# Moving the z gate's products ahead of the candidate's in a slot-attention GRU on one Trainium2 core

## What is computed

```python
for _ in range(3):
    sn = rmsnorm(slots, slot_norm_w)
    scores = einsum('bkd,bmd->bkm', sn @ Wq.T, k_proj) * SCALE
    attn = softmax(scores, axis=-2)
    attn = attn / (sum(attn, axis=-1, keepdims=True) + EPS)
    updates = einsum('bkm,bmd->bkd', attn, v_proj)
    gx, gh = updates @ wih.T + bih, slots @ whh.T + bhh
    r, z = sigmoid(xr + hr), sigmoid(xz + hz)
    n = tanh(xn + r * hn)
    slots = (1 - z) * n + z * slots
```

## Time and profile before

| | |
|---|---|
| median of 3 runs | 638.34 us (637.24 to 638.39) |
| profiled execution | 638.83 us |
| its span, first to last instruction | 637.1 us |
| PE busy | 546.8 us, 86% |
| PE weight load busy | 402.8 us, 63% |
| DVE busy | 457.4 us, 72% |
| ACT busy | 373.3 us, 59% |
| POOL busy | 253.5 us, 40% |
| mean granted TensorE clock | 0.922 |

### The profile page before, as it was taken

The page is one execution under the profiler, slowest core; times in us unless marked ns, Lnnn a source line. Parts: engine busy times, 40 slices in busy tenths (PEclk is TensorE's granted clock), DMA queues, the critical chain, the costliest instruction groups (busy, mean ns, idle before and its releaser), DMA issues.

```text
span 637.1 us, 7357 instructions
## 1 busy us (share of the span) xinstructions
PE 546.8 (86%) x2158; PEld 402.8 (63%) x2158; DVE 457.4 (72%) x806; ACT 373.3 (59%) x661; POOL 253.5 (40%) x239
## 2 busy tenths in 40 slices
PE   6999897597799979997997999799989886858781
PEld 3474536265578857876785788578878764636560
DVE  3999899985894995799489758964756579653431
ACT  4558195865665846584666668475756544634542
POOL 1032302021042564456454744543443462554453
PEclk9999897679899989998999999899999997878776
DMA  8921003010110000000000000020110724145421
GB/s 296 329 82 66 1 0 132 0 68 0 67 66 1 1 1 1 1 0 1 1 0 1 1 1 1 1 66 24 42 51 26 254 102 125 69 127 141 121 77 34
DMA packets 23896, 37.88 MB, mean 59 GB/s; under 512 B 3246, under 2 KB 15663, under 8 KB 23601
## 3 DMA queue, kind: packets, MB, share of 16 engines
q1 hardware_dynamic: 20448, 28.98, 14.5%
q0 software_dynamic: 3408, 8.43, 3.7%
HBM read 23.60 MB, written 14.72 MB: 60 GB/s over the span
## 4 chain that ended last, share of the span: by engine, by line
PE 46%; DVE 19%; issue 10%; ACT 8%; another core or an unknown queue 1%; POOL 0%; ACTq 0%; DVEq 0%; POOLq 0%
PE psum L1409 25%; PE psum L1481 7%; PE psum L1334 4%; DVE slots_full L1824 2%; DVE gru L1822 2%; DVE gru L1797 2%; PE psum L1454 2%; DVE at L1788 2%; PE psum L1158 2%; DVE sc L1779 2%; PE psum L1379 2%; DVE at L1790 2%; DVE ss_part L1755 1%; PE psum L1228 1%; PE psum L1247 1%
## 5 line engine op out<-in xcount | busy, mean ns | idle before, releaser
L1409 PE MATMUL psum<-slots_hi,w_hh 128*128 128x512 f32 x576 | 189.3, 411 | 15.3 <-DVE gru L1797 12.0
L1409 PEld LDWEIGHTS psum<-slots_hi,w_hh 128*128 128x128 f32 x576 | 109.4, 194 | 42.8 <-DVE gru L1797 13.7
L1015 POOL TENSOR_TENSOR gru<-slots_full,gru 128x512 f32<-128x512 f32 x43 | 67.8, 1576 | 161.7 <-ACT gru L744 161.6
L1409 PE MATMUL psum<-slots_lo,w_hh 128*128 128x512 f32 x288 | 116.7, 405 | 0.0
L1409 PE MATMUL psum<-at,v_ih_pair 128*128 128x512 f32 x288 | 92.9, 404 | 2.1 <-DVE at L1790 2.1
L1797 DVE SCALAR_TENSOR_TENSOR gru<-psum,vec,gru 128x512 f32<-128x512 f32 x48 | 35.9, 748 | 46.7 <-PE psum L1409 40.1
L1481 PE MATMUL psum<-slots_full,w_tile 128*128 x156 | 54.2, 482 | 14.7 <-issue 8.5
L1409 PEld LDWEIGHTS psum<-at,v_ih_pair 128*128 128x128 f32 x288 | 54.8, 193 | 17.1 <-DVE at L1790 3.9
L744 ACT ACTIVATE gru<-gru,vec 128x512 f32<-128x512 f32 x48 | 34.7, 723 | 52.3 <-DVE gru L1804 51.5
L1409 PEld LDWEIGHTS psum<-slots_lo,w_hh 128*128 128x128 f32 x288 | 55.8, 194 | 13.4
L1145 PE MATMUL psum<-early_hi,w_in 128*128 128x512 f32 x128 | 57.6, 608 | 5.1 <-DMA early_hi<-in_xT 4.9
(11 more groups left out here) (250 smaller groups left out, 1015.3 us busy)
## 6 DMA issues: line engine op xcount, KB each, us to landing
gathered<-sorted_rows SPq DMA_DIRECT2D x39, 129.0 KB, 1.9
x_scratch<-slots_full SPq DMA_DIRECT2D x8, 512.0 KB, 3.0
x_block<-x_scratch SPq DMA_DIRECT2D x8, 512.0 KB
early_hi<-in_xT SPq DMA_DIRECT2D x3, 1024.0 KB, 5.7
x_tm<-in_x SPq DMA_DIRECT2D x4, 512.0 KB, 6.9
slots_full<-in_expertT SPq DMA_DIRECT2D x1, 2048.0 KB, 11.1
sorted_rows<-gru SPq DMA_DIRECT2D x1, 1032.0 KB, 12.1
early_hi<-in_xT SPq DMA_DIRECT2D x2, 512.0 KB, 4.3
```

Source lines behind the costliest of these rows:

```text
L1015: pool.tensor_tensor(DF(u), full[:, c, seq(k, h), blk(j)], X(u), ALU.subtract).then_inc(d_pool, 1)
L1409: last = pe.matmul(psum[:, bank, :], w, d, start=start and i == 0, stop=stop and i == len(pairs) - 1)
```

## The change

In every unit the wait for `z_act` and the eight products of Z move from the end of the unit to directly behind R, and behind whatever stands in the place "R". HN, XN and their `between` places follow. The semaphores, banks and the programs of all other engines are the same.

```diff
@@ -1420,6 +1420,9 @@
                     run(R_B + u % 2, update(0), start=False).then_inc(r_mm, 1)
                     if "R" in between:
                         between["R"]()
+                    if u > 1:
+                        pe.wait_ge(z_act, u - 1)
+                    run(Z_B + u % 2, hidden(1) + update(1)).then_inc(z_mm, 1)
                     if u > 0:
                         pe.wait_ge(t_dve, u)
                     else:
@@ -1432,9 +1435,6 @@
                     run(XN_B, update(2)).then_inc(xn_mm, 1)
                     if "XN" in between:
                         between["XN"]()
-                    if u > 1:
-                        pe.wait_ge(z_act, u - 1)
-                    run(Z_B + u % 2, hidden(1) + update(1)).then_inc(z_mm, 1)
 
                 def turn(i):
```

## The result

The changed kernel took 663.51 us (median of four runs, 661.58 to 665.54) where the kernel before took 637.79 on the same chip: a ratio of 1.0407, 95% interval 1.037 to 1.0444. It is slower by 26 us. The forecast was 658.7, so the sign and most of the size are as forecast; the profiled execution has a span of 661.6 us where the one before had 637.1, a difference of 24.5.

What follows compares the result with a forecast made beforehand. PE is 86% busy; a chain of waits through the middle pairs sets their period. Profiled 638.8 + 14.0 for order (7.5 pairs, 6.5 last pair) + 6.4 for clock = 659.2; median 0.5 lower, 658.7; range 645 to 666.

Steps and rivals of the forecast that it cites:

- (d): PE's wait for `ss_low` at `mean_squares` (L1322): PE stands 1.87 us longer there, so the hand-over gain is nothing.
- rival C: Z fills the hand-over, the clock holds there and nothing takes it back: 15.6 us faster, 622.7; chance 0.04.
- The order in the pairs: Later reciprocal in unit (k,4): 1.0 us in pair 0, 1.5 in k = 1, 2, 3, 1.87 in pair 4; sum 7.5.
- The port: DVE and POOL share a port; `ss_low` may move by -0.7 to +1.0 us in each pair, taken as 0.
- the half clock behind the hand-over: Slows the 30 products behind the hand-over; without it they run into the wait for `ss_low` all the same.
- The last pair: Chains through the token tiles: three legs cost 2.3, 2.3 and 1.9 us, together 6.5.
- Order alone: Cost of the moved sets without clock effects: 7.5 in the pairs plus 6.5 in the last pair, 14.0 us.
- the third leg: Last pair, tile 18 to unit 5 and `choose(2)`: +1.9 us, at least 0 if DVE's 3.1 us idle takes it.
- The clock: Half clock behind the longer `ss_low` wait: 1.6 us four times, 6.4; last pair 0 to 2.9, taken as 0.
- the smallest seen: Clock loss per pair taken as 1.6 us, from a range of 0 to 2.9, counted four times.
- rival E: The clock is lost also in the last pair, or twice in a pair: 24.9 more, 663.2; chance 0.12.
- I expect no fall there: Hand-over stall cut into about 1.9 and 1.1 us with ten products between: no half clock, 30 products faster.

Runs made afterwards that it cites:

- e7_best: Kernel before with Z early only in unit (k,0), k > 0, `mean_squares(k+1, 3)` moved behind unit 2 and `scores(k+1)` behind HN of unit 3: 625.0 us, ratio 0.9771.
- e6_before_late: Kernel before, order of sets kept, with `mean_squares(k+1, 3)` moved behind unit 2 and `scores(k+1)` behind HN of unit 3: ratio 0.9948.
- e8_fill_all: Changed kernel plus unread products: 12 ahead of each L1322, 12 ahead of tile 0, 8 ahead of `ranks(1)` and `ranks(2)`: ratio 1.0222 to the kernel before.
- e2_last: Kernel before with Z moved ahead only in the last pair, run on the first chip: ratio 1.0159.
- e1_pairs: Kernel before with Z moved ahead only in pairs 0 to 4, the last pair keeping its order, on the first chip: ratio 1.034.
- e4_fill: Changed kernel plus 12 unread products ahead of each L1322, on the first chip: ratio 1.0344 to the kernel before.
- e5_after_late: Changed kernel with `mean_squares(k+1, 3)` moved behind unit 2 and `scores(k+1)` behind HN of unit 3: 642.65 us, ratio 1.006 to the kernel before.
- e9_handover_fill: Kernel before with Z early only in unit (k,0), k > 0, plus 12 unread products ahead of L1322: ratio 0.9999.

## Why the prediction was right in sign and low by 5 us

**The path: confirmed.** L1322 ends each pair's gain, as the prediction's (d) said. Its rival C (faster, since z fills the hand-over) named the point from which it decides, `ss_low` being ready when PE gets there; e7_best, in which PE has 16 products more ahead of it, wins 14.1 us (2.8 of them come with the move alone, e6_before_late), where C's price was 15.6. So C's mechanism was real and shut off by that one wait.

**The order in the pairs: right but for the port.** Forecast 1.0 in pair 0, 1.5 in three pairs, 1.87 in pair 4. Measured with the clock held (e8_fill_all): 1.0, 1.5, 2.5, 2.5 and 1.7. `input_part` ends and the reciprocal follows with no wait for ACT, as said; the timeline of DVE in pair 2 of the changed kernel:

```profile
332.61 0.75 DVE L1797 SCALAR_TENSOR_TENSOR gru<-psum,vec,gru 128x512 f32<-128x512 f32 x1 [1.08 <-PE psum L1409]
333.40 0.69 DVE L1804 TENSOR_TENSOR gru<-psum,gru 128x512 f32<-128x512 f32 x1
334.00 0.15 DVE L1769 RECIPROCAL small<-small 128x1 f32<-128x1 f32 x1
```

**The port: taken as 0, measured at 0.9 in each of two pairs.** The 2.5 of pairs 2 and 3 are 1.5 of order and 0.9 of this. L1322 comes 14.47 us behind HN in every pair of the changed kernel; before it was 13.55 in pairs 2 and 3 and 14.55 in pairs 1 and 4 (in pair 2 of the changed kernel counted from the release of HN). Which pairs had the longer way was not fixed: the second execution of the kernel before has 13.55 in pair 4 and 14.66 in pair 3, and with it the order comes out as 1.4 and 2.7 in these two, with nearly the same sum. In pair 4 of the first execution the 14.55 are no port: `hidden_part` of unit 1 waited 1.91 us for PE at half clock and both DVE steps took 0.7, so there the half clock behind the hand-over was on the path, against what the prediction said of it. The timelines of DVE and of POOL in pair 2 of the changed kernel:

```profile
302.71 0.75 DVE L1797 SCALAR_TENSOR_TENSOR gru<-psum,vec,gru 128x512 f32<-128x512 f32 x1
303.50 0.69 DVE L1804 TENSOR_TENSOR gru<-psum,gru 128x512 f32<-128x512 f32 x1
304.11 1.56 DVE L1822 TENSOR_TENSOR gru<-gru 128x512 f32<-128x512 f32 x1
305.70 1.64 DVE L1824 TENSOR_TENSOR slots_full<-gru 128x512 f32<-128x512 f32 x1
```

```profile
303.83 1.29 POOL L1028 TENSOR_TENSOR slots_lo<-slots_full,slots_hi 128x512 fp32r<-128x512 f32 x1
305.23 1.57 POOL L1015 TENSOR_TENSOR gru<-slots_full,gru 128x512 f32<-128x512 f32 x1
```

Both DVE steps take 0.7 us when alone; each starts while POOL is at work (303.83 to 305.12, 305.23 to 306.80) and takes over twice as long. The prediction had this inside its bounds (-0.7 to +1.0) and the case as a row; with `hidden_part` no longer waiting for PE it was the likelier end, and 0 should not have been taken. The Trainium skill ("SBUF — State Buffer", Who interferes with whom) says that whoever issues first holds the shared port for its whole instruction; the trace agrees, as POOL's start at 303.83 is ahead of DVE's at 304.11.

**The last pair: 6.5 forecast, 5.6 measured** (75.0 in e8_fill_all against 69.4). By legs the 2.3, 2.3 and 1.9 of the forecast came out as 2.7, 2.2 and 0.6: the third was near its lower bound, as the prediction allowed. The signs were partly other ones than said. Tile 0, whose wait the prediction left at 1.85, waits 3.64: between HN of unit (4,7) and tile 0 there are now eight products fewer, and `eye_and_gate` comes no sooner. Tile 11 waits 1.88, not 2.7. Tile 18 waits 0.60, not nearly 4; the wait lies ahead of it, 2.14 us in front of `ranks(1)`. Each tile that lost its cover waits 0.18 or 0.19.

**Order alone, all in all:** 14.7 against 14.0. That they are so close is partly luck: the 1.8 us of the port, taken as 0, were nearly made up by the 1.3 that the third leg did not cost.

**The clock: this step failed, by size.** Forecast 4 x 1.6 in the pairs and nothing in the last pair, 6.4. Measured 13.1: the pairs' 2.0, 2.6, 1.4 and 2.3 (each pair of the changed kernel less the same of e8_fill_all, 61.47 three times and 59.38), that is 8.3, and 4.8 behind tile 0. So "the smallest seen" was the wrong choice for the pairs, whose mean is 2.1; and in the last pair it was wrong to take 0. The prediction looked for the fall at tile 18, but the first was at tile 0, where 14 products of L1409 took 5.34 us (3.3 at the pace of 0.234): this leg lost 2.6 us to the clock. The next was behind tile 11's wait of 1.88 us, which cost the second leg 1.6 (21.18 against 19.62); e2_last has the same half clock there and the same 21.15. Tile 18 too ran at half clock (532.88, 1.25 us for its four), and the last leg lost 0.6. What happened is rival E (the clock lost also in the last pair), priced at 663.2, with a chance of 0.12. That its price meets the 663.5 measured is partly luck: it has 10.9 for the clock.

"I expect no fall there" at the hand-over was wrong as well, in two pairs of four. In pairs 2 and 3 the half clock came already behind the idle time of 1.95 us in front of the `at` products, and the ten products up to HN took 3.98 and 3.73 us (294.85 - 290.87, 358.70 - 354.97) instead of 2.3; so the second idle time, 1.15 and 1.14 us in pairs 1 and 4, is gone there. It cost nothing, since the wait at L1322 swallows it. e1_pairs, with the same order in the pairs on another chip, lost the clock at the same two. In e8_fill_all, e4_fill and e5_after_late, where no wait at L1322 before it had been long, idle times of 1.94 to 2.20 us in front of the `at` products had full clock behind them in all four pairs. Tile 11 shows the same: its wait of 1.86 to 1.89 us had half clock behind it in the changed kernel, e2_last, e4_fill and e5_after_late, and full clock in e8_fill_all, while the 1.85 at tile 0 of the kernel before had full clock. What decides is thus not the length of this stall alone, and the prediction's two stalls of 1.62 and 1.85 us with full clock were no warrant for the others; the runs don't show what else. The Trainium skill ("TensorE: Matmul & The Clock Gate", What's actually happening) says that the gate's phase is not tied to the kernel. The changed order doesn't bear that out here, as three executions lost the clock at the same two hand-overs and kept it at the same two; the kernel before may, as the half clock behind its fourth hand-over lasted longer in one execution (32 products in 10.36 us) than in the other (30 in 8.82).

**Sum.** 14.7 + 13.1 = 27.8; less 0.6 for the start of the units and 2.7 behind `turn(1)`, stages that the change does not touch, 24.5. 638.8 and 24.5 are the 663.4 of the profiled execution. The start of the units varied from 162.2 to 165.5 us over all the profiles, so of the 2.7 nothing is claimed. That the 25.7 us between the medians lie nearer to the forecast 20.4 than the 27.8 do is luck: the other comparison gave 28.7.

**Left open.** What decides whether a stall of about 1.9 us costs the clock; and what the whole change costs on the first chip, where neither it nor the kernel before was profiled. By the medians its parts add up to 20.6 + 10.2 = 30.8 us there, more than the 25.7 and 28.7 measured on the others.

## What to carry to other kernels

Work moved into an idle stretch only brings its engine sooner to its next wait: before moving it, find that wait and what releases it, and move the two together; here the one edit lost 7 us, the other won 2 to 3, and both won 14. A wait of TensorE made longer was paid twice here, in what it delays and in the half clock behind it, so a stall that moves from a place with slack to one on the path costs though PE idles no longer in all. Parts measured on different chips add up only stage by stage, for stages that are alike on both. And where an engine's waits double in the page (L1797, 40 to 79 us), ask which of them has a close second releaser behind it: 0.34 us of slack at one reciprocal decided 1.5 us a pair.

## What the runs showed of the hardware

- Unread products are faster than idling: 12 of them (2.8 us of PE's time) in a wait of 4.2 to 4.4 us made a pair 1.4 to 2.6 us shorter, though the wait ended no sooner.
- An idle time of 1.95 us in front of the `at` products had half clock behind it in six of twelve cases, the same two pairs in each of three executions (the changed kernel twice, e1_pairs), and idle times of 1.94 to 2.20 us there in none of twelve where the waits at L1322 were filled or short (e4_fill, e8_fill_all, e5_after_late).
- An idle time of 1.86 to 1.89 us at tile 11 had half clock behind it in five executions and full clock in one, e8_fill_all; 1.85 to 1.87 us at tile 0 had full clock in the kernel before and e2_last.
- A DVE step of 0.69 us took 1.54 to 1.84 us where it started 0.01 to 0.5 us behind a POOL operation of the same shape, in both kernels, e4_fill, e5_after_late, e8_fill_all and e9_handover_fill.
- The same kernel took 621.3 us on one chip and 637.7 and 638.6 on two others. The pairs of the same order were alike to 0.1 us, but for the two that differ between the two executions of the kernel before; what differs lies behind `turn(1)`, which took 87.3 to 88.2 us in the four kernels profiled on the first chip and 98.6 to 102.5 in nine profiles on the others, and from tile 18 to `turn(1)`, 25.7 us with the old order against 28.4 to 29.9. With the kernel before at 621.3 us, what it had there could only be worked out, not read.
